# Copies of adapter factors held back until two weight loads have landed, and their source buffers moved

## Chip, cores and metric

One core of one Trainium2 chip. The metric is the device time of one execution in microseconds. The profile shows one further execution, taken with the hardware profiler on.

## The reference, cut to what matters

Eight batches of 128 tokens and 512 features go through two layers in fp32; each layer adds its result to its input.

```
# layer 1, per batch b
c0 = x[b] @ W0[id[b]].T                          # 512x512, W0 picked by index
y  = c0 @ W1.T + bias + (c0 @ A0[b].T) @ B0[b].T # rank 16 adapter
x1 = x[b] + y
# layer 2
c1 = x1 @ W2.T + b2 + scale[b] * (x1 @ A1[b].T) @ B1[b].T
H  = c1 @ W3.T + b3 ; z = c1 @ A
w  = routing weights from H[:, odd tokens, :8] and z @ LiMEs.T,
     each divided by its largest absolute value over all batches, softmax, soft top 2
out = x1 + H + (z * (w @ LiMEs)) @ Bmat * scaling    # w of an odd token serves its even neighbour too
```

## The kernel before, in words

Everything is done as fp32 split into a high and a low part (fp32r), so a product is three matmuls: high by high, high by low, low by high. ACT makes the high part (a cast), VectorE the low part (a subtraction). W2 and W3 are multiplied into one matrix at the start. Batches go in pairs (NP = 4 pairs, G = 4 groups of 32 adapter rows).

Each engine runs an order written out by hand, with semaphores. TensorE's order for pair i is `layer_a` (c0 of a batch; it needs both halves of that batch's W0 as `w_hi` and `w_lo`, 6 matmuls of 512 columns for each half), `turn_c0` (four transposes of c0), `layer_low0` and `layer_low1` (8 matmuls each, of 256 columns), and `layer_b(i, h)` (26 matmuls each, two of them with the second factor `b0`). From batch 4 on the order is: layer_a(4), layer_low0(1), layer_low1(0), layer_b(1, 0), turn_c0(4), layer_a(5), layer_b(1, 1), turn_c0(5), layer_a(6), layer_low0(2), layer_low1(1), layer_b(2, 0).

The raw weights W0 come by indirect DMA from GpSimd's queue (q0 of the profile), 1 MB for each batch in two halves (`load_w`, L327), into a ring of three slots; a load waits for the casts of the load three before it. `w_landed[b][h]` counts the landing. Everything else comes through SyncE's queue (q1), in the order in which SP's instructions stand, and an SP wait holds everything behind it:

1. W1, then eight copies of `b0` parts, then x of pair 2, then eight copies more, then x of pair 3 (`load_x`, L256).
2. Sixteen copies of `be` parts, then `late_t` (bias, Bmat, selection table), then W3 again (L301), then the outputs.

`spread` (L278) is such a copy: it lays 32 rows of a second factor, found in SBUF by pairs, over the four groups of partitions. Each call issues four DMAs from SBUF to SBUF, of 64 KB for `b0` and 69 KB for `be`. The sources are scratch: `b0_parts` lies in half of `c0_lo`, and `be_parts` in `low1_t`. So whoever overwrites these must first wait for the copies: VectorE's `c0_low(2)` for all of `b0`, ACT's `low1_high(0)` (L399) for all of `be`.

ACT's order around the change is: save_c0(3), w_high(4) (two halves, L372), x1_high(0, 0), c0_high(3), x1_high(0, 1), a small cast, w_high(5), save_c0(4), low0_high(1), low1_high(0), x_high(3), w_high(6), c0_high(4), x1_high(1, 0), save_c0(5) (L413), c0_high(5), x1_high(1, 1), w_high(7), save_c0(6), low0_high(2). VectorE's is: w_low(4), x1_low(0, 0), x1_sum(0, 1), c0_low(3) (L535), x1_low(0, 1), a small one, w_low(5) with low0_low(1) between its halves, low1_low(0), x1_sum(1, 0), x_low(3), c0_low(4), w_low(6), x1_low(1, 0), x1_sum(1, 1), c0_low(5), x1_low(1, 1), w_low(7) with low0_low(2) (L545) between its halves. `layer_b(2, 0)` needs low0_low(2) for its 13th matmul.

Of the kernel before, what the change touches and what calls it, by code (L numbers as in the profile page):

```python
# [6 lines left out]
F32R = mybir.dt.float32r  # L7
# [5 lines left out]
P = 128  # L13
# [5 lines left out]
NB, S, D = 8, 128, 512  # L19
C = D // P  # L20
NP = NB // 2
# [4 lines left out]
NS = R + NE  # L26
# [12 lines left out]
G = 4  # L39
# [4 lines left out]
def width(pack):  # L44
    return sum(pack.values())
# [10 lines left out]
def build(nc, x, W0, W1, W23, g0, g1, scale, early, late, out):  # L56
    ctx = ExitStack()
    with ctx:
        def sb(name, shape, dt=F32):
            return ctx.enter_context(nc.sbuf_tensor(name, shape, dt))  # L60

        def sem(name):
            return ctx.enter_context(nc.semaphore(name))
# [14 lines left out]
        c0_hi = sb("c0_hi", [P, 2, C, 2 * S], F32R)  # L78
        c0_lo = sb("c0_lo", [P, 2, C, 2 * S], F32R)
        low0 = sb("low0", [P, 2 * S], F32R)  # L80
        low1_t = sb("low1_t", [P, 2 * (D + NS)], F32R)
        a0 = sb("a0", [P, C * NP, G, 2 * RANK], F32R)
        a1 = sb("a1", [P, C * NP, G, 2 * RANK], F32R)
        b0 = sb("b0", [P, NP, D], F32R)
# [7 lines left out]
        late_t = sb("late_t", [P, width(LATE)])  # L92
# [36 lines left out]
        def flat(ap):  # L129
            return ap.rearrange("p c s -> p (c s)")  # L130

        b1_hi = flat(c0_hi[:, 1, 0:2]).rearrange("p (c k) -> p c k", k=K1)
        b1_lo = flat(c0_hi[:, 1, 2:4]).rearrange("p (c k) -> p c k", k=K1)
        b0_parts = flat(c0_lo[:, 1]).rearrange("p (t d) -> p t d", t=2)
        low1 = low1_t[:, 0:NB * S].rearrange("p (b s) -> p b s", s=S)
        be_parts = low1_t[:].rearrange("p (t d) -> p t d", t=2)
        small_parts = flat(be[:])[:, 0:2 * C * NS].rearrange("p (c n) -> p c n", c=C)


# [22 lines left out]
        w_landed = [[sem(f"w_landed{b}_{h}") for h in range(2)] for b in range(NB)]  # L162
# [5 lines left out]
        b0_landed, be_landed = [sem(f"b0_landed{i}") for i in range(NP)], sem("be_landed")  # L168
# [11 lines left out]
        a1_ready, a1_hi_done, a1_done = sem("a1_ready"), sem("a1_hi_done"), sem("a1_done")  # L180
# [36 lines left out]
        def columns(step):  # L217
            return slice(0, D) if step < NB - 1 else slice(D // 2 * (step - NB + 1), D // 2 * (step - NB + 2))

        def f32(ap):  # L220
            return ap.bitcast(F32)
# [9 lines left out]
        def w_slot(b):  # L231
            n = order.index(b)
            return (n + 2) % RING
# [19 lines left out]
        @engines.sync  # L253
        def _(sp):
            def load_x(i):
                sp.dma_start(flat(x_in[:, i]), x[i]).then_inc(x_landed[i], 16)  # L256

            def load_w23(c):
                at = 2 * D * (c % 2)
                sp.dma_start(w_in[:, c // 2, at:at + 2 * D], W23[c]).then_inc(w23_landed[c], 16)  # L260

            sp.dma_start(w_in[:, 0, D:2 * D], W23[0][:, D:2 * D]).then_inc(w23_landed[0], 16)
            load_w23(1)
            load_w23(2)
            load_w23(3)
            load_x(0)
            load_x(1)
            slot, half = w_slot("w1"), C * D // 2
            sp.wait_ge(w2_lo_done, 4)
            sp.wait_ge(w3_lo_done, 4)  # L270
            for h in range(2):
                sp.dma_start(w_in[:, slot, half * h:half * (h + 1)],
                             W1[:, half * h:half * (h + 1)]).then_inc(w1_landed[h], 16)

            def spread(t, parts, i, landed):

                for g in range(G):
                    sp.dma_start(f32(t[K2 * g:K2 * (g + 1), i]),  # L278
                                 f32(parts[K2 * i:K2 * (i + 1), 0 if g < G - 1 else 1])).then_inc(landed, 16)

            sp.wait_ge(b0_hi_done, 1)
            sp.wait_ge(b0_done, 1)
            spread(b0, b0_parts, 0, b0_landed[0])
            spread(b0, b0_parts, 1, b0_landed[1])
            sp.wait_ge(a0_ready, 1)
            load_x(2)
            spread(b0, b0_parts, 2, b0_landed[2])
            spread(b0, b0_parts, 3, b0_landed[3])
            sp.wait_ge(a1_ready, 1)
            load_x(3)  # L290
            sp.wait_ge(be_hi_done, 1)
            sp.wait_ge(be_done, 1)
            sp.wait_ge(bes_hi_done, 1)
            sp.wait_ge(bes_done, 1)
            for i in range(NP):
                spread(be, be_parts, i, be_landed)
            sp.dma_start(late_t[:], late).then_inc(late_landed, 16)

            sp.wait_ge(w_hi_done, 2 * W3_AFTER + 2)
            sp.wait_ge(w_lo_done, 2 * W3_AFTER + 2)  # L300
            sp.dma_start(w3_again, W23.rearrange("c p n -> p c n")[:, :, D:]).then_inc(w3_landed, 16)  # L301
            for step in range(NB + 1):
                b, at = min(step, NB - 1), columns(step)
                sp.wait_ge(out_done, step + 1)
                sp.dma_start(out[b][:, at], out_sb[:, b % 4, at]).then_inc(out_stored[b % 4], 16)
            for n in range(4):
                sp.wait_ge(out_stored[n], 32 if n < 3 else 48)
# [52 lines left out]
        def _(act):  # L360
# [33 lines left out]
            def low1_high(i):  # L394
                act.wait_ge(low1_ready, i + 1)
                if i == 0:
                    act.wait_ge(be_landed, 16 * NP * G)
                for j in range(2):
                    last = nc.scalar.activation(low1[:, 2 * i + j], bank[7][:, S * j:S * (j + 1)], ACT.Copy,  # L399
                                                scale=block[:, j:j + 1])  # L400
                last.then_inc(low1_hi_done, 1)
# [77 lines left out]
            for i in range(2, NP):  # L479
                w_high(2 * i + 1)  # L480
                save_c0(2 * i)
                low0_high(i - 1)
                low1_high(i - 2)
                if i + 1 < NP:
                    x_high(i + 1)
                    w_high(2 * i + 2)
                c0_high(2 * i)
                x1_high(i - 1, 0)
                save_c0(2 * i + 1)
                c0_high(2 * i + 1)  # L490
                x1_high(i - 1, 1)
            low0_high(NP - 1)
            low1_high(NP - 2)
            x1_high(NP - 1, 0)
            x1_high(NP - 1, 1)
            act.wait_ge(bw_step, C)
            nc.scalar.copy(bw_hi, bw).then_inc(bw_hi_done, 1)
            act.wait_ge(late_landed, 16)
            nc.scalar.copy(bm_parts[:], bm4).then_inc(bm_hi_done, 1)
            low1_high(NP - 1)  # L500
            act.wait_ge(bias_ready, 1)
            nc.scalar.copy(bias_all, bank[7][:]).then_inc(bias_done, 1)
# [13 lines left out]
        def _(dve):  # L516
            def x_low(i):
                dve.wait_ge(x_hi_done, i + 1)
                nc.vector.tensor_tensor(x_lo[:, i], x_in[:, i], f32(x_hi[:, i]), ALU.subtract).then_inc(x_lo_done, 1)
# [11 lines left out]
            def c0_low(b):  # L531
                if b >= 4:
                    dve.wait_ge(y_ready, 2 * (b // 2 - 1))
                dve.wait_ge(c0t_hi_done, b + 1)
                nc.vector.tensor_tensor(tok(c0_lo[:, (b // 2) % 2], b),  # L535
                                        bank[2 + b % 2][:].rearrange("p (c s) -> p c s", s=S),
                                        f32(tok(c0_hi[:, (b // 2) % 2], b)), ALU.subtract).then_inc(c0t_lo_done, 1)
# [155 lines left out]
            nc.vector.tensor_tensor(a1[:, :, 0], pairs(bank[5][:]), f32(a1[:, :, 1]), ALU.subtract).then_inc(a1_done, 1)  # L693
            x1_sum(0, 0)
            x_low(2)
            for i in range(NP):
                dve.wait_ge(b0_landed[i], 16 * G)
            c0_low(2)
            w_low(4)
            x1_low(0, 0)  # L700
# [125 lines left out]
            for step in range(NB + 1):  # L826
                b, at = min(step, NB - 1), columns(step)
# [349 lines left out]
```

## Time and profile before

| | |
|---|---|
| runs without the profiler | 125.0, 125.01, 128.61 us, median 125.01 |
| profiled execution, its own time | 126.08 us |
| its span | 123.7 us |
| TensorE busy | 117.6 us (95%), mean granted clock 0.986 |
| VectorE, ACT, GpSimd busy | 82.6, 56.5, 24.9 us |
| chain that ended last | PE 78%, DMA 10%, ACT 4%, DVE 4% |

The span runs from the first to the last instruction on the chip; 2.4 us of the profiled execution's time lie around it. All times in the views count from the start of the span. The chain that ended last is followed back from the end, so what stands in it ahead of a TensorE stretch is what that stretch waited for.

### The profile page before, as it was taken

The page shows a single profiled execution, that of the slowest core. Times are in us where ns is not written, and L with a number is a line of the kernel's source. Part 1 is how long each engine was busy: PE and PEld are TensorE (multiplying, and loading weights), DVE is VectorE, ACT ScalarE, POOL GpSimd, SP SyncE. Part 2 cuts the span into 40 slices and gives each one's busy share as a digit, 9 for nine tenths or more (in the row PEclk, how much of TensorE's full clock was granted, in tenths as well). Part 3 has the DMA queues.
Part 4 walks back from the last instruction along what each step waited for, and adds up shares of the span by engine and source line. Part 5 has one row for each costly group of instructions (what it writes and reads, how often), then busy time and mean ns, then how long its engine had stood idle before and what let it go on. Part 6 is the DMA issues. An engine that isn't in the chain of part 4 may idle for free.

```text
span 123.7 us, 1917 instructions
## 1 busy us (share of the span) xinstructions
PE 117.6 (95%) x703; PEld 101.1 (82%) x703; DVE 82.6 (67%) x170; ACT 56.5 (46%) x93; POOL 24.9 (20%) x30
## 2 busy tenths in 40 slices
PE   6999999999999975999999999999999999999991
PEld 2588878888898964998989989999989687688890
DVE  0599996895979719757796841779765476503661
ACT  4388667869788434909549040330620100230000
POOL 3077884060068703301300000000000000000000
PEclk9999999999999998599999999999999999999999
DMA  3999999859978999999500000000000000000872
GB/s 117 400 417 341 402 331 402 341 133 294 262 187 237 317 284 309 312 337 400 203 5 0 0 0 0 0 5 0 0 0 0 5 0 0 0 0 0 309 274 99
DMA packets 7864, 20.78 MB, mean 168 GB/s; under 512 B 1200, under 2 KB 1584, under 8 KB 7856
## 3 DMA queue, kind: packets, MB, share of 16 engines
q1 hardware_dynamic: 4944, 10.87, 25.9%
q0 software_dynamic: 2624, 9.44, 23.3%
q10 hardware_dynamic: 288, 0.36, 0.8%
q8 instruction: 5, 0.08, 0.3%
q14 instruction: 3, 0.02, 0.1%
HBM read 16.39 MB, written 2.10 MB: 149 GB/s over the span
## 4 chain that ended last, share of the span: by engine, by line
PE 78%; DMA 10%; ACT 4%; DVE 4%; issue 2%; POOL 0%; POOLq 0%; ACTq 0%
PE bank L841 63%; DMA w_in<-in_W,rows_i 7%; PE bank L944 3%; PE bank L947 3%; PE bank L950 3%; DMA w_in<-in_W 3%; DVE w_lo L675 2%; PE bank L878 1%; PE bank L1024 1%; ACT a L405 1%; DVE w_lo L528 1%; ACT w_hi L372 1%; ACT w_hi L378 1%; PE bank L935 1%; PE bank L1093 1%
## 5 line engine op out<-in xcount | busy, mean ns | idle before, releaser
L327 POOL DMA_INDIRECT w_in<-in_W,rows_i x16 | 18.3, 1146 | 25.5 <-DVE w_lo L528 9.5
L528 DVE TENSOR_TENSOR w_lo<-w_in,w_hi 128x1024 fp32r<-128x1024 f32 x16 | 19.3, 1225 | 5.5 <-ACT w_hi L372 4.1
L372 ACT CAST w_hi<-w_in 128x1024 fp32r<-128x1024 f32 x16 | 16.4, 1051 | 5.4 <-DMA w_in<-in_W,rows_i 5.4
L841 PE MATMUL bank<-c_hi,w_hi 128*128 128x256 f32 x64 | 18.1, 284 | 0.0
L841 PE MATMUL bank<-c_lo,w_hi 128*128 128x256 f32 x64 | 18.1, 283 | 0.0
L841 PE MATMUL bank<-c_hi,w_lo 128*128 128x256 f32 x64 | 18.1, 282 | 0.0
L841 PE MATMUL bank<-w_hi,x_hi 128*128 128x512 f32 x32 | 13.5, 421 | 2.0 <-DVE w_lo L528 2.0
L841 PE MATMUL bank<-m_hi,x_hi 128*128 128x512 f32 (+1 forms) x36 | 13.9, 386 | 0.0
L841 PE MATMUL bank<-m_hi,x_lo 128*128 128x512 f32 (+1 forms) x36 | 13.2, 368 | 0.0
L841 PE MATMUL bank<-m_lo,x_hi 128*128 128x512 f32 (+1 forms) x36 | 13.2, 367 | 0.0
L841 PE MATMUL bank<-w_hi,x_lo 128*128 128x512 f32 x32 | 12.8, 400 | 0.0
L841 PE MATMUL bank<-w_lo,x_hi 128*128 128x512 f32 x32 | 12.7, 397 | 0.0
L841 PEld LDWEIGHTS bank<-c_hi,w_hi 128*128 128x128 f32 x64 | 12.2, 191 | 0.3 <-issue 0.2
L841 PEld LDWEIGHTS bank<-c_lo,w_hi 128*128 128x128 f32 x64 | 12.2, 191 | 0.1
L841 PEld LDWEIGHTS bank<-c_hi,w_lo 128*128 128x128 f32 x64 | 12.3, 192 | 0.0
L832 DVE TENSOR_TENSOR w_in<-bank,late_t 128x512 f32<-128x512 f32 (+1 forms) x9 | 5.3, 629 | 8.0 <-PE bank L841 6.7
L579 DVE SCALAR_TENSOR_TENSOR x_in<-bank,early_t,x_in 128x256 f32<-128x256 f32 x16 | 7.0, 478 | 5.0 <-PE bank L841 5.0
L841 PEld LDWEIGHTS bank<-w_hi,x_hi 128*128 128x128 f32 x32 | 6.0, 188 | 3.4 <-issue 2.4
L424 ACT CAST x_hi<-x_in 128x512 fp32r<-128x512 f32 x8 | 5.0, 622 | 8.2 <-DVE x_in L579 8.2
L419 ACT CAST c_hi<-bank 128x512 fp32r<-128x512 f32 x8 | 4.7, 589 | 8.2 <-PE bank L878 8.2
L841 PEld LDWEIGHTS bank<-m_hi,x_hi 128*128 128x128 f32 x36 | 6.8, 188 | 1.5 <-issue 0.5
L841 PEld LDWEIGHTS bank<-m_hi,x_lo 128*128 128x128 f32 x36 | 6.8, 188 | 1.2
(177 smaller groups left out, 241.3 us busy)
## 6 DMA issues: line engine op xcount, KB each, us to landing
w_in<-in_W SPq DMA_DIRECT2D x5, 512.0 KB, 4.5
x_in<-in_x SPq DMA_DIRECT2D x4, 512.0 KB, 7.0
out_dram<-w_in SPq DMA_DIRECT2D x7, 256.0 KB, 2.9
be<-low_t SPq DMA_DIRECT2D x16, 69.0 KB
b<-c_lo SPq DMA_DIRECT2D x16, 64.0 KB, 4.4
w_in<-in_W SPq DMA_DIRECT2D x1, 1024.0 KB, 6.9
late_t<-in_late SPq DMA_DIRECT2D x1, 552.0 KB, 10.9
w_in<-in_W ACTq DMA_DIRECT2D x1, 256.0 KB, 3.5
```

Source lines behind the costliest of these rows:

```text
L327: nc.gpsimd.indirect_dma_start(w_in[:, slot, half * h:half * (h + 1)], None, W0, row).then_inc(w_landed[b][h], 16)
L372: nc.scalar.copy(part(w_hi[:, b % 2], h), raw(b, h)).then_inc(w_hi_done, 1)
L419: nc.scalar.copy(tok(c0_hi[:, (b // 2) % 2], b), bank[2 + b % 2][:].rearrange("p (c s) -> p c s", s=S)).then_inc(c0t_hi_done, 1)
L424: nc.scalar.copy(part(x_hi[:, i], h), part(x_in[:, i], h)).then_inc(x1_hi_done, 1)
L528: nc.vector.tensor_tensor(part(w_lo[:, b % 2], h), raw(b, h), f32(part(w_hi[:, b % 2], h)), ALU.subtract).then_inc(w_lo_done, 1)
L579: last = nc.vector.scalar_tensor_tensor(x_in[:, i, m], y, bias1_c[:, m:m + 1], x_in[:, i, m], ALU.add, ALU.add)
L675: nc.vector.tensor_tensor(part(w1_lo[:], h), raw("w1", h), f32(part(w1_hi[:], h)), ALU.subtract).then_inc(w1_lo_done, 1)
L832: nc.vector.tensor_tensor(out_sb[:, b % 4, at], bank[OUT_BANK[step]][:, at], bias_all[:, at], ALU.add).then_inc(out_done, 1)
L841: ins = mm(o, st, mv, start=start and n == 0, stop=stop and n == len(parts) - 1)
L944: mm(bank[m][:], chunk(w_hi[:, 1, c], m), w1_hi[:, c], start=c == 0, stop=False)
L947: mm(bank[m][:], chunk(w_hi[:, 1, c], m), w1_lo[:, c], start=False, stop=False)
L950: mm(bank[m][:], chunk(w_lo[:, 1, c], m), w1_hi[:, c], start=False, stop=False)
```

## The change

Three things are changed. The source of the `b0` copies moves to `low1_t`, that of the `be` copies to `late_t`. With that the waits move: VectorE's `c0_low(2)` waits for no copies any more, ACT's `low1_high(0)` waits for the `b0` copies instead of the `be` copies, and SP waits for the `be` copies before it loads `late_t`. And SP's order changes: after the four copies of `b0` for pair 0 and x of pair 2 it waits until both halves of W0 of batch 4 have landed, then issues four copies, x of pair 3, the other eight copies of `b0`, waits for W0 of batch 5, and then issues the `be` copies.

```diff
-        low1_t = sb("low1_t", [P, 2 * (D + NS)], F32R)
+        low1_t = sb("low1_t", [P, NB * S], F32R)
...
-        b0_parts = flat(c0_lo[:, 1]).rearrange("p (t d) -> p t d", t=2)
-        low1 = low1_t[:, 0:NB * S].rearrange("p (b s) -> p b s", s=S)
-        be_parts = low1_t[:].rearrange("p (t d) -> p t d", t=2)
+        low1 = low1_t[:].rearrange("p (b s) -> p b s", s=S)
+        b0_parts = low1_t[:].rearrange("p (t d) -> p t d", t=2)
+        be_parts = late_t[:, 0:2 * (D + NS)].bitcast(F32R).rearrange("p (t d) -> p t d", t=2)
...
             spread(b0, b0_parts, 0, b0_landed[0])
-            spread(b0, b0_parts, 1, b0_landed[1])
             sp.wait_ge(a0_ready, 1)
             load_x(2)
+            sp.wait_ge(w_landed[4][1], 16)
+            spread(b0, b0_parts, 1, b0_landed[1])
+            sp.wait_ge(a1_ready, 1)
+            load_x(3)
             spread(b0, b0_parts, 2, b0_landed[2])
             spread(b0, b0_parts, 3, b0_landed[3])
-            sp.wait_ge(a1_ready, 1)
-            load_x(3)
+            sp.wait_ge(w_landed[5][1], 16)
             sp.wait_ge(be_hi_done, 1)
...
             for i in range(NP):
                 spread(be, be_parts, i, be_landed)
+            sp.wait_ge(be_landed, 16 * NP * G)
             sp.dma_start(late_t[:], late).then_inc(late_landed, 16)
...
             def low1_high(i):
                 act.wait_ge(low1_ready, i + 1)
                 if i == 0:
-                    act.wait_ge(be_landed, 16 * NP * G)
+                    for n in range(NP):
+                        act.wait_ge(b0_landed[n], 16 * G)
...
             x_low(2)
-            for i in range(NP):
-                dve.wait_ge(b0_landed[i], 16 * G)
             c0_low(2)
```

## Rows read from the trace of the kernel before

**Rows 1.** Timeline of PE: start, duration, line, operation, tiles, count, idle before.
```profile
47.77 0.47 PE L841 MATMUL bank<-w_hi,x_hi 128*128 128x512 f32 x1 [2.02 <-DVE w_lo L528]
...
49.75 0.48 PE L841 MATMUL bank<-c_hi,a 128*128 128x256 f32 x1
```
**Rows 2.** Stretches: engines' busy us (count), then granted clock, DMA share, GB/s.
```profile
50.00:51.00 1.00, 1.00 (x6) 1.00 (x6) 0.69 (x3) 1.00 (x2) 0.58 (x1) 0.50 1.04 308
52.50:54.00 1.50, 1.50 (x15) 1.50 (x14) 1.08 (x3) 0.29 (x2) 0.00 (x0) 1.00 1.07 304
```
**Rows 3.** Chain that ended last, in order of time: start, us, what.
```profile
36.17 9.12 DMA w_in<-in_W,rows_i
...
45.31 1.06 ACT w_hi L372
...
47.77 8.19 PE bank L841 x48
...
56.40 5.85 PE bank L841 x38
62.24 0.44 PE bank L878 x4
62.68 7.74 PE bank L841 x54
```
**Rows 4.** Timeline of POOL: batch 7's first W0 load.
```profile
48.39 0.94 POOL L327 DMA_INDIRECT w_in<-in_W,rows_i  x1 [5.13 <-DVE w_lo L528]
```
**Rows 5.** DMA queues from 48 to 52 us: packets, MB, share of 16 engines.
```profile
q0 software_dynamic: 241, 0.88, 73.1%
q1 hardware_dynamic: 237, 0.35, 31.4%
```
**Rows 6.** Stretch of 36 to 38 us, columns as in rows 2.
```profile
36.00:38.00 2.00, 2.00 (x19) 2.00 (x18) 1.83 (x2) 2.00 (x3) 1.52 (x2) 1.00 0.67 175
```
**Rows 7.** DMA issues at 17.94, 24.49 and 25.73 us: last number is us to landing.
```profile
w_in<-in_W,rows_i POOLq DMA_INDIRECT x1, 6.0
w_in<-in_W,rows_i POOLq DMA_INDIRECT x1, 4.7
w_in<-in_W,rows_i POOLq DMA_INDIRECT x1, 7.6
```
**Rows 8.** Line L278, the copies: issue durations, and DMA to landing.
```profile
L278 SPq DMA_DIRECT2D b<-c_lo x16: 507/591/1167, 24.4 to 35.0; - x16
L278 SPq DMA_DIRECT2D be<-low_t x16: 527/591/1052, 36.4 to 46.5; - x16
...
DMA to landing us min/median/max: 4.2/4.4/4.7
```
**Rows 9.** Timeline of SP's queue: x of pair 3.
```profile
35.63 0.58 SPq L256 DMA_DIRECT2D x_in<-in_x  x1
```
**Rows 10.** Timeline of ACT.
```profile
41.40 1.05 ACT L372 CAST w_hi<-w_in 128x1024 fp32r<-128x1024 f32 x1
...
49.79 1.99 ACT L372 CAST w_hi<-w_in 128x1024 fp32r<-128x1024 f32 x2
...
55.62 0.63 ACT L399 ACTIVATE low_t<-bank,block 128x128 fp32r<-128x128 f32 x2 [2.83 <-DMA be<-low_t]
...
59.97 0.60 ACT L413 COPY c_row<-bank 128x512 f32<-128x512 f32 x1
```
**Rows 11.** Timeline of DVE.
```profile
48.92 0.68 DVE L535 TENSOR_TENSOR c_lo<-bank,c_hi 128x512 fp32r<-128x512 f32 x1
...
60.27 2.35 DVE L528 TENSOR_TENSOR w_lo<-w_in,w_hi 128x1024 fp32r<-128x1024 f32 x2
...
67.68 0.61 DVE L545 SCALAR_TENSOR_TENSOR low<-bank,block,low 32x128 fp32r<-32x128 f32 x2 [0.72 <-ACT low L391]
```
**Rows 12.** Timeline of PE: first matmul that reads the third pair's low-rank product.
```profile
68.59 0.28 PE L841 MATMUL bank<-low,b 128*128 128x256 f32 x1
```
**Rows 13.** Timeline of DVE: first reader of `late_t` and of W3.
```profile
82.43 0.75 DVE L732 SCALAR_TENSOR_TENSOR c_row<-w_in,early_t,late_t 128x512 f32<-128x512 f32 x1
```

## Prediction

> **What bounds the kernel now.** I read the page first: TensorE is busy for 95% of the span, so only what makes it idle or slow is worth anything. Its timeline shows one idle stretch over 1 us once it has started: 2.02 us ahead of the second half of layer_a(4), released by the low part of W0 [rows 1]. The chain gives the reason: the second half of batch 4's W0, issued at 36.17, landed 9.12 us later; the cast (45.31) and the subtraction followed, and TensorE went on at 47.77 [rows 3]. The stretches add a second loss: soon after the idle time the granted clock was 0.50 (1.2 GHz), and it was back at 1.00 (2.4 GHz) by 52.5 [rows 2]. The chain prices this. The 48 matmuls from 47.77 took 8.19 us. The block of 54 from 62.68 took 7.74 and has the same make-up with 6 more of 512 columns at the full clock [rows 3]; those 6 take 1.4 us (5.85 us for 38 in the block from 56.40, of which 26 of 256 columns take 3.1, leaves 2.75 for 12). So the 48 would take 6.35, and the low clock cost 1.85. The whole wait is worth 2.02 + 1.85 = 3.9 us, 3% of the time, the most that this change can bring.
>
> The next thing to read is who else is close behind. ACT's low1_high(0) began at 55.62, after 2.83 us of waiting for the be copies [rows 10]. From there ACT and VectorE run almost without a pause: save_c0(5) ends at 60.57 [rows 10], the low part of W0 of batch 6 is made from 60.27 to 62.62, its first half by about 61.45, and low0_low(2) ends at 68.29 [rows 11]. TensorE needs these at 62.24, 62.68 [rows 3] and 68.59 [rows 12]. The slack is 1.7, 1.2 and 0.3 us. So when low1_high(0) starts later than 55.62, nearly all of it reaches the end; and when it does not start earlier, TensorE cannot end more than some 0.2 us earlier (0.3 less about 0.1 for a semaphore), whatever it gained before.
>
> **The W0 load of batch 4.** The change empties SP's queue of eleven or more copies and of x of pair 3 while this load is in flight. Three other half loads bound its landing: 4.7 us (the queue of GpSimd idle before, little traffic), 6.0 (another), 7.6 (second half, beside b0 copies and x of pair 2) [rows 7]. I take 6.0, since ours is a second half too, behind the first by 1.2 us, but without the traffic. With 36.17 that is T = 42.2, between 40.9 and 43.8. ACT is free for this cast 0.95 us after it began the first half at 41.40 [rows 10], so 42.35: T is just early enough. Before, layer_low0(1) began 4.44 us after the landing (49.75 against 45.31), because VectorE must get through x1_sum(0, 1) and c0_low(3), which ended at 49.60 [rows 1, 3, 11]. With 42.35 that gives 46.8, plus 0.35 since VectorE is busy with the first half: 47.15, about when TensorE comes there by itself. TensorE's gain by turn_c0(5) is 3.9 less up to 0.5 for low0_low(1), which moves only by the 2.7 us of VectorE and ACT: 3.4 us. TensorE arrives there at 62.24 - 3.4 = 58.8.
>
> In a sentence apart: the Trainium skill (DMA: Bandwidth & Descriptors, Anatomy of one DMA) has a fit of 2.0 us plus bytes/436e3 for a DMA from GpSimd, 3.2 us for 512 KB; no half load read here was that quick (the best is 4.7 us), and by it everything behind T would come 2.8 us earlier.
>
> **The copies, now behind T.** At T SP issues four copies of b0, x of pair 3, and eight copies. An issue takes 0.59 us in the median [rows 8], so the thirteen take 7.7 us, the last one starting at T + 7.1. A copy issued into a quiet queue landed after 4.4 us [rows 8]. The lower bound is T + 11.5. But the queue is not quiet: GpSimd's queue has batches 5, 6 and 7 to bring, 3 MB. From 48 to 52 us both queues were full; q0 had 241 packets and q1 237, the DMA share was over 1, and q1 moved only 0.35 MB [rows 2, 5]. That is 59 packets a us on q1. A copy of 69 KB takes 0.8 us then, that is 48 packets; a b0 copy has as many rows, so I give it 0.8 us too. Twelve make 9.7 us. x of pair 3 in rows of 4 KB has about 144 packets, 2.4 us. Sum 12.1 us. What comes on top (first packet, landing, the slowest of the 16 engines) I take from the be copies of before: from the issue of x of pair 3 at 35.63 [rows 9] to the landing at 55.62 [rows 10] are 20.0 us, and 16 copies and x by the same rates make 15.3. So at most 4.7, part of which was a backlog of earlier copies. I take 2.4. Y, the time at which low1_high(0) may start, is T + 14.5 = 56.7. Its bounds are 40.9 + 11.5 = 52.4 and 43.8 + 16.8 = 60.6.
>
> So the wait at low1_high(0) is not removed. It was for 16 copies issued from 36.4, and is now for 12 copies, 8 of them issued from about 45 on. It starts earlier (ACT arrives at about 50.1 instead of 52.8) and ends 1.1 us later. Queued behind it on ACT are x_high(3), w_high(6), c0_high(4), x1_high(1, 0) and save_c0(5), and on VectorE low1_low(0) with all that follows.
>
> **What that makes of the end.** With Y = 56.7 save_c0(5) ends at 61.7. TensorE, at turn_c0(5) since 58.8, idles some 2.9 us; then the first half of w_low(6) lets it go at 62.65. After the 2.02 us of before the clock fell; an idle stretch that is longer, with 0.4 us more behind it, is likely to do the same. From 62.68 to 68.59 it had 5.9 us of work; with 1.8 for the clock it reaches low0 at 70.4, against 69.5 for low0_low(2) (68.29 + 1.1 + 0.1). The end moves by 70.4 - 68.6 = **+1.8 us**. Without the low clock it would be +0.9.
>
> **Edits at nothing.** x of pair 2 is issued 2.8 us earlier, four copies ahead; ACT had no wait for it. b0 for pair 1 lands at T + 1.3 + 3.3 + 0.8, about 47.6, up to 49.5 at the late bound, and layer_b(1, 0) needs it at about 49; a small wait there is swallowed by the idle time at 58.8. x of pair 3 is ahead of the last copies, so within Y. VectorE's removed wait had cost nothing before. W0 of batches 5 and 6 lands earlier than before or as before, and W0 of 7, issued after w_low(4) [rows 4], some 2.7 us earlier. The be copies are issued from about 50 to 60 and land by 65; late_t, queued behind the added SP wait, lands by about 70 (10.9 us before, now with no other traffic), and W3 behind it by 73. The first reader of both is at 82.43 [rows 13]; TensorE waits for be only after its block that ends at 70.4 [rows 3]. That leaves 5 us for be and 9 for the others; if it were gone, each us would show in the tail, since the bias is made from both.
>
> **Profile and runs.** The profiled execution took 126.08 us with a span of 123.7; the median without the profiler is 1.07 lower. I add the difference to the median: 125.0 + 1.8 = **126.8 us**. A measurement of this kernel can tell about 2%, 2.5 us, from no change.
>
> **Rivals.** (a) *The copies land early.* If T is near 41 and the queues share better than in [rows 5], Y comes to 54 or less; then the chain behind low1_high(0) moves forward by 1.6, TensorE hardly idles, and the clock holds: 125.0 - 1.6 - 0.2 = 123.2. For it: SP can issue all in 7.7 us, and q0 has had its batch 5 in part by T. Against: 3 MB on q0 keep both queues full until about 55. A gain over 2.5 us needs Y at 53.2, close to its bound.
> (b) *The copies land late, and the clock falls.* In this case the end moves by 0.7 + (Y - 55.6), so from Y = 57.4 on the kernel is slower by over 2.5 us; at Y = 58.5, with T at 43 and an overhead of 3.4 instead of 2.4, it gives 125.0 + 3.6 = 128.6. For it speaks the one measured case, in which 4.7 us came on top.
> (c) *The load isn't held by the traffic.* From 36 to 38 us, with the next SP transfers hardly begun, the DMA share was only 0.67 at 175 GB/s [rows 6], against 308 GB/s in [rows 2]: the load was then limited by how fast GpSimd's queue was fed, not by others. If so T stays near 45.3, the old wait of 2.02 and its clock loss remain, Y is 59.8, and the end moves by over 4 us: about 129.5. The Trainium skill (SBUF — State Buffer, Who interferes with whom) says that VectorE holds up GpSimd's descriptors in its two-port modes of copy, cast and tensor_scalar, and not in tensor_tensor; the VectorE work of 36 to 38 us, w_low(3), is of the tensor_tensor kind [rows 11], so by that page VectorE is not what starved it, and no run here shows what did. Against (c): the 6.0 and 4.7 us of [rows 7] were under such feeding too.
>
> **Chances.** Forecast, Y from 54.8 to 57.4: 0.50. Rival (a), below that: 0.20, of which 0.07 is a gain over 2.5 us. Rival (b) 0.23, rival (c) 0.07. Faster by over 2%: 0.07; slower by over 2%: 0.23 + 0.07 = 0.30; the rest, 0.63, within. The range runs from 123.4 (most of (a)) to 128.8 (most of (b)) and leaves out (c) and the ends, 0.17 in all. The forecast's own range is 124.8 to 127.5.
>
> **What the profile after would show.** Right: no idle time of TensorE at 45.8; the copies' first issue after the first wait near 42; ACT's L399 starting at 56 to 57, released by the b copies; TensorE idle ahead of the L878 transposes near 59 for 2 to 3 us, and a granted clock of 0.50 after it. Wrong if L399 starts before 54 (rival a), if TensorE still waits for w_lo at 45.8 (rival c), or if TensorE waits somewhere else, such as for be, late_t or W3 in the tail.

## The result, and the profile after

The changed kernel took 128.76 us in the median of four runs (128.17 to 129.13). The kernel before, run again beside it, has now 125.79 us (125.0 to 128.61, four runs). The ratio is 1.025, with a 95% interval of 1.014 to 1.036: slower by 1.4 to 3.6%. Ratios here and below leave out runs that took over 1.5% longer than the fastest run of the same kernel. The forecast was 126.8 us, so the sign was right and the size too small; what happened is nearest to rival (b), the late copies, to which the text gave a chance of 0.23.

The profiled execution took 129.13 us with a span of 127.4, against 126.08 and 123.7 before. The difference of the spans, 3.7 us, is what has to be explained; the four runs have spans of 126.4 to 127.4. TensorE's timeline, with the idle time ahead of an instruction in brackets, has three waits between 40 and 80 us:

```profile
52.25 0.36 PE L847 MATMUL bank<-c_hi,w_hi 128*128 128x256 f32 x1 [3.02 <-DMA b<-low_t]
64.32 0.66 PE L884 MATMUL bank<-ident,c_row 128*128 128x128 f32 x4 [0.93 <-ACT c_row L421]
65.34 0.47 PE L847 MATMUL bank<-w_hi,x_hi 128*128 128x512 f32 x1 [0.36 <-DVE w_lo L536]
```

The wait of before for W0 of batch 4 [rows 1] is gone. In its place stands one of 3.02 us ahead of layer_b(1, 0), for the copies of b0 for pair 1. Two short ones follow ahead of turn_c0(5) and layer_a(6). The clock fell once, after the first of these (the third number from the end is the granted clock):

```profile
50.00:52.00 2.00, 0.00 (x0) 0.00 (x0) 1.67 (x3) 0.20 (x1) 0.00 (x0) 1.00 1.02 288
52.00:54.00 2.00, 1.75 (x10) 1.78 (x11) 0.17 (x1) 0.00 (x0) 0.00 (x0) 0.69 1.05 314
54.00:56.00 2.00, 2.00 (x11) 2.00 (x10) 0.00 (x0) 0.00 (x0) 0.00 (x0) 0.50 1.01 306
56.00:58.00 2.00, 2.00 (x15) 1.91 (x15) 0.00 (x0) 0.00 (x0) 0.00 (x0) 0.95 1.08 246
```

By these rows the low clock (1.2 GHz) took 0.6 + 1.0 + 0.1 = 1.7 us from TensorE. So TensorE traded 2.02 + 1.85 for 3.02 + 1.7, which by itself would make the kernel 0.9 us slower. It is 3.7 us slower. The chain that ended last (start, us, what) shows that TensorE isn't even on it from 36 to 65 us:

```profile
36.27 5.29 DMA w_in<-in_W,rows_i
41.57 0.02 issue
41.59 0.51 SPq L281
...
49.80 9.42 DMA b<-low_t
...
59.95 0.93 ACT x_hi L370
...
63.98 1.23 DVE w_lo L536
65.20 0.14 issue
65.34 2.99 PE bank L847 x12
...
71.38 0.62 DVE low L553 x2
72.00 0.04 issue
72.05 1.93 PE bank L847 x14
```

It goes from the landing of W0 of batch 4 (41.57, where [rows 3] had 45.29) through SP's issues to the last b0 copy, issued at 49.80 and landed 9.42 us later. Then come ACT and VectorE. ACT's timeline shows the same:

```profile
49.57 0.62 ACT L398 ACTIVATE low<-bank,block 128x128 fp32r<-128x128 f32 x2
59.32 0.63 ACT L407 ACTIVATE low_t<-bank,block 128x128 fp32r<-128x128 f32 x2 [9.13 <-DMA b<-low_t]
```

L407 is low1_high(0), which had started at 55.62 [rows 10]. It is 3.7 us later, and so is all that hangs on it: the first matmul that reads the third pair's low-rank product is at 72.05 instead of 68.59 [rows 12], 3.5 us later, and the span is longer by 3.7. In the tail neither be, late_t nor W3 made TensorE wait. The second wait that the change gives SP, for W0 of batch 5, held nothing: SP issued the first be copy at 50.57, right behind the last b0 copy, and its waits show only one for a W0 load, the 13.7 us before 41.59.

### The profile page after: what moved, and what is told of

It is laid out like the page before. It is cut to its first block, busy times and chain, and to the rows that moved or that the text cites. A ratio compares the mean times of both kernels' runs of the same rounds, so it can differ in the third digit from the quotient of the medians.

```text
span 127.4 us, 1916 instructions
## 1 busy us (share of the span) xinstructions
PE 119.1 (94%) x703; PEld 101.8 (80%) x703; DVE 82.7 (65%) x170; ACT 56.5 (44%) x93; POOL 24.4 (19%) x30
## 4 chain that ended last, share of the span: by engine, by line
PE 66%; DMA 12%; ACT 7%; SPq 6%; DVE 4%; issue 3%; POOL 0%; ACTq 0%; DVEq 0%; POOLq 0%
PE bank L847 49%; DMA b<-low_t 7%; SPq L281 5%; DMA w_in<-in_W,rows_i 4%; PE bank L960 3%; PE bank L950 3%; PE bank L953 3%; PE bank L956 3%; DVE w_lo L683 2%; ACT w_hi L379 2%; PE bank L1030 1%; ACT a L413 1%; DVE w_lo L536 1%; ACT c_hi L427 1%; ACT w_hi L385 1%
## 5 line engine op out<-in xcount | busy, mean ns | idle before, releaser
L847 PE MATMUL bank<-c_hi,w_hi 128*128 128x256 f32 x64 | 18.9, 295 | 3.0 <-DMA b<-low_t 3.0
L847 PE MATMUL bank<-c_lo,w_hi 128*128 128x256 f32 x64 | 18.8, 293 | 0.0
L847 PE MATMUL bank<-c_hi,w_lo 128*128 128x256 f32 x64 | 18.7, 293 | 0.0
L847 PEld LDWEIGHTS bank<-c_hi,w_hi 128*128 128x128 f32 x64 | 12.9, 202 | 3.5 <-issue 3.3
L847 PEld LDWEIGHTS bank<-c_lo,w_hi 128*128 128x128 f32 x64 | 12.9, 202 | 0.1
L847 PEld LDWEIGHTS bank<-c_hi,w_lo 128*128 128x128 f32 x64 | 12.9, 202 | 0.0
L562 DVE SCALAR_TENSOR_TENSOR low_t<-bank,block,low_t 32x128 fp32r<-32x128 f32 x8 | 2.5, 344 | 9.1 <-ACT low_t L407 9.0
```

The lines of the kernel that those rows point to most:

```text
L847: ins = mm(o, st, mv, start=start and n == 0, stop=stop and n == len(parts) - 1)
```

## The experiments

Three theories stood. **Late copies:** the end follows the start of low1_high(0), which waits for the last b0 copy. **First wait:** the cost is TensorE's 3.02 us for pair 1 and the low clock behind it. **Load not held:** holding SP back doesn't bring W0 of batch 4 earlier. All kernels compute the whole reference. All edits are to the changed kernel.

**r1_sources.** SP's order of before, with the new sources and places of waits. (The diffs of SP's order, here and below, don't show waits that stay beside their transfer.)

```diff
             spread(b0, b0_parts, 0, b0_landed[0])
+            spread(b0, b0_parts, 1, b0_landed[1])
             load_x(2)
-            sp.wait_ge(w_landed[4][1], 16)
-            spread(b0, b0_parts, 1, b0_landed[1])
-            load_x(3)
             spread(b0, b0_parts, 2, b0_landed[2])
             spread(b0, b0_parts, 3, b0_landed[3])
-            sp.wait_ge(w_landed[5][1], 16)
+            load_x(3)
```

> Only the new source buffers and the moved waits, with SP's order of the kernel before and no wait for W0. Three theories stand. 'Late copies': the end follows the start of ACT's low1_high(0) (L407), which waits for the last b0 copy (59.3 us after the change). 'First wait': the cost is TensorE's 3.02 us ahead of layer_b(1, 0) and the low clock behind it. 'Load not held': holding SP back doesn't bring W0 of batch 4 earlier for its own sake. Late copies: the copies land near 40, low1_high(0) starts at about 52.8 without a wait, TensorE waits for W0 at 45.8 for 2.0 us as before, and since TensorE then runs without a pause nothing is gained: span 123.4 to 123.8. First wait: the same span. Load not held: the same.

Measured: ratio to the kernel before 0.9996 (0.995 to 1.004), ten runs. low1_high(0) started at 52.17 without a wait, TensorE waited 1.06 us for W0 of batch 4 and the clock didn't fall (span 122.9). So the moved sources and waits alone neither cost nor bring anything: without ACT's 2.83 us of waiting at 52.8 [rows 10] the kernel is no faster.

**r2_pair1_early.** Pair 1's copies issued before the wait.

```diff
             load_x(2)
-            sp.wait_ge(w_landed[4][1], 16)
             spread(b0, b0_parts, 1, b0_landed[1])
+            sp.wait_ge(w_landed[4][1], 16)
```

(The copies stand ahead of load_x(2), as before.)

> The change, but the four copies of pair 1 are issued ahead of the wait for W0 of batch 4, as in the kernel before. Late copies: TensorE's wait ahead of layer_b(1, 0) goes, and the last b0 copy lands some 2.5 to 3.3 us earlier, near 56.4; the end moves with that alone, span 124.1 to 124.9, and by 1:1 with the start of low1_high(0). First wait: the span falls by the wait and its clock loss, 3.0 + 1.7, to about 122.7, whatever low1_high(0) does. Load not held: as late copies.

Measured: its four runs scatter from 124.84 to 129.23 us (median 127.66), so no ratio is given. The profile is of a run of 127.22 us. TensorE's timeline and the clock:

```profile
51.17 0.39 PE L846 MATMUL bank<-low,b 128*128 128x256 f32 x1 [0.28 <-DVE low L552]
61.83 1.02 PE L883 MATMUL bank<-ident,c_row 128*128 128x128 f32 x4 [2.43 <-ACT c_row L420]
```
```profile
62.00:64.50 2.50, 2.50 (x8) 1.84 (x8) 2.50 (x4) 0.58 (x1) 0.29 (x1) 0.50 0.97 343
```

The first wait is gone, but this execution's span, 125.5, is still longer than before, and over the expected 124.1 to 124.9. TensorE waits 2.43 us at turn_c0(5) instead, the place that the prediction had named, and the clock falls there. low1_high(0) started at 56.83. That speaks against First wait, which asked for 122.7, but doesn't settle it: the fastest of the four runs had a span of 123.1 and a mean granted clock of 1.000, which is nearer to 122.7, and no trace of it shows when its copies landed. r9_no_low1_wait decides.

**r3_b0_early.** All b0 copies before the wait, x of pair 3 and be behind it.

```diff
             load_x(2)
+            spread(b0, b0_parts, 2, b0_landed[2])
+            spread(b0, b0_parts, 3, b0_landed[3])
             sp.wait_ge(w_landed[4][1], 16)
             load_x(3)
-            spread(b0, b0_parts, 2, b0_landed[2])
-            spread(b0, b0_parts, 3, b0_landed[3])
```

(Pair 1's stand ahead of load_x(2).)

> All sixteen b0 copies are issued ahead of the wait for W0 of batch 4 (order of the kernel before); only x of pair 3 and the be copies stand behind it. Late copies: low1_high(0) starts near 50.2 without a wait, TensorE has neither the wait at 45.8 nor the one at 49.2, and the span is 120.3 to 121.5; the next thing late may be x of pair 3, issued near 42. First wait: the same sign, span about 122. Load not held: the second half of W0 of batch 4 lands at 44 or later, TensorE waits at 45.8, span 123.5.

Measured: ratio 0.980 (0.972 to 0.987), median 123.29. low1_high(0) started at 50.96 with no wait, and the only idle time of TensorE that its timeline shows from 36 to 82 us is 0.29 us. The span is 121.7, 0.2 above the expected range; at its start the first four matmuls after the warm-up took 1.84 us until the next ones began, against 1.01 in the changed kernel, which is 0.8 us at a place that the edit does not touch. So what harmed was holding back b0; with only x and be behind the load the kernel gains. First wait asked for about 122, so this run doesn't separate the two.

**r4_gates_off.** SP's order of the change, neither wait for W0.

```diff
-            sp.wait_ge(w_landed[4][1], 16)
...
-            sp.wait_ge(w_landed[5][1], 16)
```

> SP's order of the change, without its two waits for W0. Late copies: b0 copies land by 42, low1_high(0) doesn't wait; W0 of batch 4 has traffic beside it again (copies of pair 3 and be), so its second half lands at 43 to 46 and TensorE waits 0 to 2 us at 45.8: span 121.5 to 124. First wait: the same, since that wait is gone too. Load not held: the landing is that of the change, 41.6, and the span about 120.5.

Measured: ratio 0.992 (0.988 to 0.997), ten runs. TensorE waits again for W0 of batch 4, 1.26 us; ACT began its second half at 45.56, when the load landed, 8.7 us after its issue. low1_high(0) had no wait (52.93). Load not held, which asked for an unchanged landing, falls.

**r7_gate_be_only** asks which traffic had held the load.

```diff
             spread(b0, b0_parts, 2, b0_landed[2])
             spread(b0, b0_parts, 3, b0_landed[3])
+            load_x(3)
+            sp.wait_ge(w_landed[4][1], 16)
-            sp.wait_ge(w_landed[5][1], 16)
...
             for i in range(NP):
                 spread(be, be_parts, i, be_landed)
```

(The wait and load_x(3) at their old places, ahead of these, are gone, and pair 1's copies stand ahead of load_x(2).)

> All b0 copies early as in the kernel r3_b0_early, but x of pair 3 is issued early too, and only the be copies wait for W0 of batch 4. It asks which traffic had held W0 of batch 4. Late copies: low1_high(0) waits for nothing. If x of pair 3 (512 KB beside the load) was what held it, the second half lands at 44 or later and TensorE waits 1 us at 45.8, span 122.5 to 123.5; if it was the be copies, it lands at 42 to 42.5 and the span is 120.6 to 121.7.

Measured: ratio 0.973 (0.961 to 0.984), median 123.34. x of pair 3 was issued at 35.91, the second half of W0 of batch 4 at 36.85; it landed after 6.1 us and TensorE had no wait for it. With the be copies beside it too it had taken 8.2 us (r1_sources), 8.7 (r4_gates_off) and 9.12 [rows 3]. r7_gate_be_only and r1_sources have the same SP order but for the wait ahead of be, so the be copies made the load 2.1 us late there, and x of pair 3 next to nothing: with x held back as well the load took 5.8 us (r3_b0_early). The span of the profiled execution, 122.6, lies in the range that was given for the other answer; the other three runs had 121.3 to 121.9. It is the landing, and TensorE not waiting, that answer the question.

The next four take the wait at low1_high(0) away, or shorten it.

**r9_no_low1_wait** and **r10_no_low1_wait_pair1.** The source of the b0 copies lies where nobody writes before they land, so ACT needs no wait; only the be copies that write this place wait for them. The order of the b0 copies is that of the change in r9; in r10 pair 1's are issued early, as in r2_pair1_early.

```diff
-        b0_parts = low1_t[:].rearrange("p (t d) -> p t d", t=2)
+        b0_parts = flat(be[:])[:, D + NS:D + NS + 2 * D].rearrange("p (t d) -> p t d", t=2)
...
-                    for n in range(NP):
-                        act.wait_ge(b0_landed[n], 16 * G)
...
-            for i in range(NP):
+            for i in (0, 3, 1, 2):
+                if i == 1:
+                    for n in range(NP):
+                        sp.wait_ge(b0_landed[n], 16 * G)
                 spread(be, be_parts, i, be_landed)
```

> The change, with the source of the b0 copies in the middle of the be tile, so that ACT's low1_high(0) waits for no copies; SP's order is that of the change (only the be copies into that place wait until the b0 copies have landed). TensorE's wait for pair 1's copies stays. Late copies: low1_high(0) starts at about 50, TensorE keeps its 3.0 us ahead of layer_b(1, 0) and 1.7 us of low clock behind it, and starts layer_b(1, 0) about when it did before: span 123.3 to 125.2. First wait: nothing changes, 127.4. Load not held: as late copies.

> As the run before it, and pair 1's copies are issued ahead of the wait for W0 of batch 4. Late copies: no wait is left, though eight b0 copies still land near 56.8; the span is 121.0 to 122.0, like that of the kernel with all b0 copies early (121.7). First wait: the same.

Measured: r9 0.996 (0.991 to 1.001), r10 0.970 (0.963 to 0.978), median 122.81. TensorE's and ACT's timelines of r9:

```profile
52.35 0.36 PE L847 MATMUL bank<-c_hi,w_hi 128*128 128x256 f32 x1 [2.51 <-DMA b<-be]
```
```profile
50.68 0.63 ACT L407 ACTIVATE low_t<-bank,block 128x128 fp32r<-128x128 f32 x2
54.89 1.05 ACT L373 CAST x_hi<-x_in 128x1024 fp32r<-128x1024 f32 x1 [3.59 <-DMA x_in<-in_x]
```

TensorE keeps its wait for pair 1, 2.51 us at the same place and time, and ACT waits 3.59 us for x of pair 3, issued behind the same wait of SP. Yet the span is 123.6 and not 127.4, and the ratio is that of no change. In this execution the clock didn't fall behind TensorE's wait, which could be taken for part of the gain; but four further runs whose mean granted clock was 0.983 to 0.985, like the changed kernel's 0.987, had spans of 123.8 to 124.4, 2 to 3.6 us under the changed kernel's 126.4 to 127.4. So taking away ACT's wait gives back the loss with TensorE's wait left in place, and First wait falls. The remaining four of the ten runs had spans of 126.1 to 127.2; what made them long isn't known, and their clock, 0.983 to 0.986, doesn't set them apart. In r10 the last copy still lands only 8.5 us after its issue at 47.5, nearly as long as the 9.42 us of the changed kernel, but nobody waits for it; the span is 120.6, the shortest of all.

**r6_x3_early** and **r8_w6_w7_later** are about the landing of the copies. r6 issues x of pair 3 ahead of the wait; r8 leaves SP as it is and holds GpSimd's loads of batches 6 and 7 until the copies have landed:

```diff
+                if b == NB - 2:
+                    pool.wait_ge(b0_landed[3], 16 * G)
                 half = C * D // 2
```

> The change, with x of pair 3 issued ahead of the wait for W0 of batch 4. Late copies: the queue behind the wait is shorter by its 144 packets, so low1_high(0) starts 2.5 to 3 us earlier than 59.3, near 56.6, and the span is 127.4 less the same, 124.4 to 125.5 (up to 0.9 more with a low clock late). First wait: the span stays at 127, since the pair 1 wait stays. Load not held: W0 of batch 4 lands when it did.

> The change, with GpSimd's loads of W0 of batches 6 and 7 held until the last b0 copy of pair 3 has landed, so that the copies share the DMA engines only with what is left of batch 5. It is for the landing of the copies, not for the time. If the shared engines make the copies late, the last b0 copy lands at 53.5 to 55.5 instead of 59.2 and low1_high(0) starts then; if it is SP's own issue rate and order, it stays near 59. W0 of batch 6 will then be late for ACT, landing near 60, so the span is 126 to 128 either way.

Measured, r6: low1_high(0) at 57.57, span 125.7; one run of 127.38 us. The start moved by 1.75 us and the span by 1.7, which is the one to one of late copies. The queue behind the wait is shorter by x. SP's wait ended at 42.21 in this run and at 41.59 in the changed kernel, so counted from there low1_high(0) starts after 15.4 us instead of 17.7: 2.4 us less, which is what the 144 packets were to take.

Measured, r8: low1_high(0) at 52.21, after a wait of 1.35 us. SP's issues are as late as in the change (the wait ends at 42.4, the last copy is issued at 50.1), and yet all has landed 7 us earlier. Line L281 of r8, and under it of the changed kernel:

```profile
DMA to landing us min/median/max: 1.9/3.4/4.5
```
```profile
DMA to landing us min/median/max: 2.6/6.0/10.6
```

(Each view is of all copies of the line, b0 and be.) So of the changed kernel's 17.65 us from the landing of W0 of batch 4 to the last landing, 9.8 are there in r8 too, the first 7.7 of them until SP begins to issue the last copy, and the other 7.9 are the company of the 2 MB of batches 6 and 7. r8's own time (129.32 us in one run, span 127.5) shows the other side: ACT then waits 4.47 and 1.69 us for W0 of batch 6.

**r11_b0_early_no_low1_wait** is r3_b0_early with the source of r10.

> All b0 copies early, and their source in the be tile, so that both repairs are made at once. If the late copies were the whole cause, the second repair has nothing left to mend: the time is that of either repair alone, 122.3 to 123.4 us, span 120.6 to 121.7.

Measured: 0.968 (0.958 to 0.979), median 122.92. The profiled span was 122.3, over the expected 120.6 to 121.7; the other four runs had 120.8 to 121.4. The intervals of r3, r7, r10 and r11 overlap, so no gain of the second repair over one alone can be seen. Each of the four is faster than the kernel before, by 2 to 3%; only in r10 does the whole interval lie below 0.98.

The end against the start of low1_high(0), in the profiled executions in which the copies bind:

| kernel | low1_high(0) starts | span | 123.7 + (start - 55.62) - 0.2 |
|---|---|---|---|
| change | 59.32 | 127.4 | 127.2 |
| r6_x3_early | 57.57 | 125.7 | 125.45 |
| r2_pair1_early | 56.83 | 125.5 | 124.7, and a low clock behind the wait |
| r1_sources | 52.17 | 122.9 | doesn't bind |
| r3_b0_early | 50.96 | 121.7 | doesn't bind |

## Why the prediction was wrong in its size

**Right.** That TensorE had up to 3.9 us to gain: in r10, where it waits for nothing over 0.3 us, the span is 3.1 us shorter than before. But of this sum the 1.85 us of low clock were TensorE's loss; the kernel's runs don't show them. Of the 19 runs of the kernel before beside r1 to r4, eighteen had a mean granted clock of 0.998 to 1.000 and spans of 123.4 to 125.9; the nineteenth had 0.985, like the profiled one, and 123.7. That fits the chain behind low1_high(0), which had only 0.3 us of slack. T, forecast at 42.2, was 41.57. The chain behind low1_high(0) with slacks of 1.7, 1.2 and 0.3 us, and that its wait isn't removed but moved: [rows 10 and 11] had shown it, and the last column of the table is its formula. The be copies, late_t and W3 had the slack that was claimed. The measured 128.76 us lies inside the stated range of 123.4 to 128.8, but at its very end.

**The step that failed** is the time of the copies: "What comes on top (first packet, landing, the slowest of the 16 engines) [...] I take 2.4", and with it Y = T + 14.5. It was T + 17.65, so Y was 59.2 and not 56.7; the sum's largest term was short by 3.15 us, of which 0.6 came back from T. The step took q1's share of the DMA engines, 59 packets a us [rows 5], from the first moment on. But those rows were of a time at which both queues had long been full. Right behind the wait it was different. The queues' packets in the changed kernel from 42 to 45 us, then from 45 to 48:

```profile
q0 software_dynamic: 186, 0.66, 80.3%
...
q0 software_dynamic: 187, 0.70, 80.0%
q1 hardware_dynamic: 103, 0.14, 13.4%
```

The first copy was issued at 41.59, and for 3 us q1 has no row at all; by 48 it had moved 103 of the 720 packets that the prediction counted, where 59 a us from T + 1.3 on would have made 300. In r8, without the loads of batches 6 and 7, it had moved 49 and 253 in the same stretches, though its first copy was issued 0.8 us later, at 42.43:

```profile
q0 software_dynamic: 203, 0.72, 77.6%
q1 hardware_dynamic: 49, 0.07, 6.4%
...
q1 hardware_dynamic: 253, 0.64, 71.2%
q0 software_dynamic: 35, 0.11, 13.0%
```

So the delay belongs to the presence of the two loads that GpSimd issued around T (at 41.03 and 42.42). Why q1 gets nothing at first, though later it moves as many packets as q0, no run here tells, and it stays open. The slow start is not the whole of the 3.15 us either. From 48 to 56 us q1 moved 528 packets, 66 a us and thus more than the 59; by 56.5 it had moved 714, some of be's among them, which by the prediction's rate was due at about 55. But the last b0 copy landed only at 59.22, 2.7 us after that, by when be copies from behind it in the queue had landed. In r8 the 720 packets and the last landing came together, at 52.1. By these counts about half of the error is the start and about half the tail of the last copies, and both are gone without GpSimd's loads of batches 6 and 7. What came on top of the 12.1 us measured 5.5: it was outside the bound of 4.7 as well, and Y stayed within its own bound of 60.6 because that bound also allowed for a T as late as 43.8.

**The second step that failed** is "b0 for pair 1 lands at T + 1.3 + 3.3 + 0.8, about 47.6". TensorE had it at 52.25, after the same slow start of q1. That the wait would be "swallowed" was right for the end, as r9 shows, but it moved the clock's fall: the forecast had it at 59 to 62, at a price of 0.9 us. It fell at 53, where TensorE had 1.3 us to spare afterwards (0.93 + 0.36), and cost the end nothing. With the measured Y and the forecast's own rule for a low clock, the end would have moved by 0.7 + 3.6 = 4.3 us; without it by 3.4. It moved by 3.5 at low0 and 3.7 in all. In r2_pair1_early, where the wait was at 59.4 to 61.8, the clock did fall where it was forecast, and cost 0.8.

**The lower bound** of Y, T + 11.5, was too high: r8 reached T + 9.8. Its last b0 copy, issued at 50.13, landed 2.0 us later, and not 4.4.

**Rival (c)** spoke from [rows 6], a DMA share of 0.67 with the next SP transfers hardly begun. But 70 of the 134 packets of that stretch were already on SP's queue. In the changed kernel, where q0 was alone, the share was lower still (0.52 from 36 to 38 us), and the load came 3.8 us sooner once SP's transfers were held back (r7: 3.0 us with be alone held back). The Trainium skill's rule that VectorE's tensor_tensor doesn't hold up GpSimd's descriptors (SBUF — State Buffer, Who interferes with whom) was not tried by any run here.

## What to carry to other kernels

Before holding transfers back for one that is late, ask of each of them who waits for it, and how much of the chain behind that wait is slack. Here the be copies were issued 14 us later than before and TensorE never waited for them; the last eight b0 copies were issued nearly 15 us later, and ACT waited 9.13 us. Both had been put behind the same wait. Small copies that will share the DMA engines with a large load are best issued before it is queued, as in r3 and r7; r8 shows that they land early without the load as well, but then the load is late for others. And price a burst of copies from a stretch in which it starts, not only from one in which both queues have long been running, and add what the slowest copy takes after the last packet is due.

## What was not expected of the hardware

**The queue that starts second.** SP's first copy was issued at 41.59 us, while GpSimd's queue was busy and had 1 MB more just coming. On SP's queue no packet moved before 45.2, 3.6 us later. In r6 nothing moved from 42.21 to 46.7 and in r9 from 42.58 to 47.5, 4.5 and 4.9 us. With batches 6 and 7 held back (r8) the first packets came 2.0 us after the issue, though q0 moved 66 packets a us meanwhile in both kernels. Of the changed kernel's copies of line L281 the median took 6.0 us to land and the longest 10.6; of r8's the median took 3.4.

**What a load pays for its company.** Beside the second half of W0 of batch 4, from its issue to its landing, SP's queue moved 0.19 MB in r3, 0.53 MB in r7 and 0.96 MB in r1, and the load took 5.8, 6.1 and 8.2 us. Both queues together moved 0.29 MB a us in r3 and r7 and 0.28 in r1. So x of pair 3 cost the load almost nothing, and the further 0.43 MB at r7's rate make some 1.5 us (an estimate) of the 2.1 that the be copies cost it. That small copies cost a load more than their bytes is therefore not shown.

**The clock after an idle stretch isn't a matter of its length alone.** TensorE idled 2.51 us in r9 and 2.54 us in r6, at the same place. In r9 the clock stayed at 1.00 in every stretch from 50 to 58 us, in r6 it fell:

```profile
54.00:56.00 2.00, 2.00 (x20) 2.00 (x19) 0.27 (x1) 1.11 (x2) 0.00 (x0) 1.00 1.02 305
```
```profile
53.00:56.00 3.00, 3.00 (x18) 3.00 (x18) 0.00 (x0) 0.00 (x0) 0.00 (x0) 0.61 1.05 288
```

The kernel before, run 19 times beside the first experiments, took 125.09 to 127.68 us. The clock is not the reason for that: the five runs over 127 us had a mean granted clock of 0.999 or 1.000. What is stays open.
